# Row sums as two columns, inverted there and spread by two turns; masked scores kept in PSUM; the tail in another order

## What is computed

```
q, k, v   from projections; q and k through rms_norm, own q and k through rope
scores  = q @ [k_ctx, k_self]^T                 (causal on the 256 own keys)
weights = softmax(scores / sqrt(128))           (max over the 4352 keys subtracted)
out     = weights @ [v_ctx, v_self];   x1 = x + concat(heads) @ wo
```

## Time and profile before

| | |
|---|---|
| Median of 3 executions | 1031.19 us (1029.86 to 1032.27) |
| The profiled execution, its own time | 1030.32 us |
| Its span, first to last instruction | 1028.3 us |
| Lies around the span | 2.0 us |
| PE busy with matmuls | 986.7 us, 96% of the span |
| DVE, ACT, POOL busy | 788.0, 586.2, 517.4 us |
| Mean granted TensorE clock | 0.995 of 2.4 GHz |

### The profile page before, as it was taken

One profiled execution on the slowest core, in us unless ns is written; L12 is line 12 of the kernel. 1 busy time (PEld: TensorE's weight loads), 2 busy tenths in 40 slices (PEclk: granted clock), 3 DMA queues, 4 the chain that ended last, 5 costly groups with the idle time before them and its releaser, 6 DMA issues.

```text
span 1028.3 us, 15218 instructions
## 1 busy us (share of the span) xinstructions
PE 986.7 (96%) x5597; PEld 856.8 (83%) x5597; DVE 788.0 (77%) x1168; ACT 586.2 (57%) x962; POOL 517.4 (50%) x481
## 2 busy tenths in 40 slices
PE   8999999998899999999999999989799999999998
PEld 7888888888888888888888888877587988888887
DVE  6645666547988888888988888889479978777775
ACT  5444434345665666656666656655279576666664
POOL 4543344330777778787777787779201032222222
PEclk9999999999999999999999999989999999999999
DMA  7647564377005020221105030040540486555540
GB/s 281 195 145 224 195 205 133 114 256 239 2 8 167 22 67 1 83 92 42 47 1 171 5 89 4 2 185 1 205 164 2 155 316 216 190 192 189 194 157 20
DMA packets 52488, 127.89 MB, mean 124 GB/s; under 512 B 3872, under 2 KB 32960, under 8 KB 50880
## 3 DMA queue, kind: packets, MB, share of 16 engines
q1 hardware_dynamic: 52416, 126.94, 36.3%
HBM read 99.64 MB, written 27.30 MB: 123 GB/s over the span
## 4 chain that ended last, share of the span: by engine, by line
PE 76%; DVE 17%; issue 3%; POOL 2%; DMA 1%; ACT 0%; DVEq 0%; SPq 0%; POOLq 0%
PE bank L523 17%; PE bank L627 13%; PE bank L505 13%; PE bank L597 12%; PE bank L905 9%; DVE run_max L1065 5%; PE bank L907 5%; DVE run_max L1055 4%; DVE weights L1085 3%; POOL run_sum L1864 2%; PE bank L713 1%; PE bank L532 1%; DVE run_max L1062 1%; DMA w_xa<-in_w_in 1%; DVE weights L1052 1%
## 5 line engine op out<-in xcount | busy, mean ns | idle before, releaser
L1864 POOL TENSOR_TENSOR run_sum<-run_sum,weights 128x512 f32<-128x512 f32 x224 | 292.9, 1307 | 52.2 <-ACT weights L1581 32.7
L627 PE MATMUL bank<-weights,vN 128*128 128x256 f32 (+1 forms) x1088 | 316.2, 378 | 0.0
L597 PE MATMUL bank<-qT_hi,kT 128*128 128x256 f32 (+1 forms) x1088 | 300.9, 360 | 2.1 <-ACT weights L1577 1.2
L597 PEld LDWEIGHTS bank<-qT_hi,kT 128*128 128x128 f32 x1088 | 198.4, 189 | 25.9 <-issue 2.4
L1577 ACT COPY weights<-bank 128x512 f32<-128x512 f32 x256 | 148.8, 585 | 123.0 <-PE bank L597 114.0
L1065 DVE TENSOR_TENSOR run_max<-bank,run_max 128x512 f32<-128x512 f32 x200 | 137.2, 686 | 55.8 <-ACT weights L1577 55.4
L627 PEld LDWEIGHTS bank<-weights,vN 128*128 128x128 f32 x1088 | 173.0, 190 | 4.2
L1581 ACT ACTIVATE weights<-weights 128x1024 f32<-128x1024 f32 x144 | 144.0, 1001 | 54.8 <-DVE weights L1085 54.8
L1085 DVE TENSOR_TENSOR weights<-weights,bank 128x1024 f32<-128x1024 f32 x128 | 154.8, 1210 | 3.2 <-PE bank L655 3.2
L597 PE MATMUL bank<-qT_lo,kT 128*128 128x256 f32 (+1 forms) x544 | 153.4, 282 | 0.0
L523 PE MATMUL bank<-w_ctx_hi,ctx_hl 128*128 128x512 f32 x512 | 144.5, 393 | 1.5 <-ACT w_ctx_hi L1543 1.3
(11 more groups left out here) (236 smaller groups left out, 1514.3 us busy)
## 6 DMA issues: line engine op xcount, KB each, us to landing
e_raw<-in_experts SPq DMA_DIRECT2D x51, 768.0 KB, 4.4
k_spill<-k_stage SPq DMA_DIRECT2D x16, 1024.0 KB, 5.3
kT<-k_spill SPq DMA_DIRECT2D x15, 1024.0 KB, 5.2
v_spill<-v_stage SPq DMA_DIRECT2D x16, 512.0 KB, 6.4
vN<-v_spill SPq DMA_DIRECT2D x16, 512.0 KB, 3.6
ctx_raw<-in_ctx SPq DMA_DIRECT2D x15, 512.0 KB, 4.1
w_raw<-in_w_qkv SPq DMA_DIRECT2D x6, 1024.0 KB, 5.1
wo_sb<-in_wo SPq DMA_DIRECT2D x4, 1024.0 KB, 7.8
```

The costliest lines, as they stand in the source:

```text
L597: done = e.matmul(dst, kT[:, w, kt * P:(kt + 1) * P], qT[a][:, h, q0:L], start=m == 0, stop=m == 2)
L627: done = e.matmul(dst[:, q0:L], vN[:, kt, :].bitcast(F32), weights[:, cols], start=kt == 0, stop=kt == KTILES - 1)
L1864: e.tensor_tensor(run_sum[:, :], run_sum[:, :], here, ALU.add).then_inc(summed, 1)
```

## The change

Between the two kernels, all in the attention part and its tail:
- **Masked group**: DVE adds the mask in place in the PSUM bank, takes both maxima from there, and only then ACT copies the group to SBUF like any other (`take_scores` waits for `maxed`).
- **Order in a step on DVE**: the subtraction ahead of the running maximum; subtractions 5 and exponentials 3 steps ahead instead of 6 and 4. `fold_max` stands in the step of the head's last group instead of at k = 0 and is a reduction over the two halves instead of a `tensor_tensor`.
- **Later turns**: `turn_max`, `reduce_rows`, `spread_max` at k = 4, 5, 6 instead of 2, 3, 5 (first head: 6, 7, 8).
- **Row sums**: at k = 1 PE waits for a new ACT copy of the head's output to SBUF (`copy_out`, 128x256), then makes the sums as two columns (two fp32 products with a one-column operand); DVE inverts 128x2 at k = 2; PE spreads the two columns by two transposes at k = 3; DVE multiplies at k = 4; ACT and POOL finish at k = 5 and 6.
- **Last head's sums**: POOL adds groups 0 to 3, DVE the other 13 (`add_own_weights`), PE joins both in the sums.
- **Tail**: `w_xa`, `w_xb` and the small weights are loaded when the last head's scoring starts, `wo` in five parts while it is scored (`WO_LOADS`, `WO_ORDER`); `wo` is split from step 246 and multiplied from 249. The additions to `x` and the normalisations stand ahead of the pairs' low parts on DVE.
- Code for a split of weights that was never on (`SPLIT = {}`) is taken out.

```diff
-SUB_AHEAD, EXP_AHEAD, SPLIT_AHEAD = 6, 4, 2
+SUB_AHEAD, EXP_AHEAD, FINISH_LAG = 5, 3, 2
+TURN_AT, REDUCE_AT, SPREAD_AT = (6, 4), (7, 5), (8, 6)
-WO_STEP, WO_PRODUCTS = 250, 253
+OWN_SUMS = 4
+WO_STEP, WO_PRODUCTS = 246, 249
+WO_LOADS = (((0, 2), (9, 10)), ((2, 4), (10, 12)), ((4, 6), (12, 14)), ((6, 8), (14, 16)), ((8, 9),))
+WO_ORDER = (0, 1, 9, 2, 3, 10, 11, 4, 5, 12, 13, 6, 7, 14, 8, 15)
...
             def sum_weights(h):
-                pe.wait_ge(summed, SUMS * (h + 1))
-                e.matmul(bank[VALUE_BANKS[h % 2]][:, L:2 * L], ones[:, :], both_sum[:, :], start=True, stop=True).then_inc(sum_all, 1)
+                pe.wait_ge(out_copied, h + 1)
+                parts = [(both_sum, (summed, SUMS * (h + 1) if h < H15 else SUMS * H15 + OWN_SUMS))]
+                if h == H15:
+                    parts.append((own_both, (own_summed, SUMS - OWN_SUMS)))
...
+                for qt in range(TT):
+                    for i, (part, ready) in enumerate(parts):
+                        done = e.matmul(bank[VALUE_BANKS[h % 2]][:, L + qt:L + qt + 1], part[:, qt * P:(qt + 1) * P], ones[:, 0:1],
+                                        start=i == 0, stop=i == len(parts) - 1)
+                done.then_inc(sum_all, 1)
+            def spread_sums(h):
+                pe.wait_ge(ho, 2 * h + 1)
+                for qt in range(TT):
+                    done = e.transpose(bank[VALUE_BANKS[h % 2]][:, L + qt * P:L + (qt + 1) * P], rden[:, qt:qt + 1].to_broadcast([P, P]), ident[:, :])
+                done.then_inc(sum_all, 1)
...
                 h, k = divmod(n - NG, NG)
-                if k == 0 and h in range(H15):
+                if k == 1 and h in range(H15):
                     sum_weights(h)
+                if k == 3 and h in range(H15):
+                    spread_sums(h)
...
             sum_weights(H15)
-            for h in range(5):
+            project_out(1, 0)
+            project_out(1, 1)
+            spread_sums(H15)
+            for h in range(2, 5):
                 project_out(1, h)
             project_out(0, H15)
...
                 if g == SELF:
-                    wait_slot(dve, h, g)
-                    e.tensor_tensor(slot[:, g, 0:L + P], src[:, 0:L + P], causal[:, :], ALU.add).then_inc(maxed, 1)
+                    dve.wait_ge(scored, s + 1)
+                    e.tensor_tensor(here[:, 0:L + P], here[:, 0:L + P], causal[:, :], ALU.add).then_inc(maxed, 1)
                     for k, (to, lo, n) in enumerate(((0, 0, L), (P, L, P))):
...
-                        e.tensor_tensor(run_max[:, to:to + n], run_max[:, to:to + n], slot[:, g, lo:lo + n], ALU.max).then_inc(maxed, 1)
+                        e.tensor_tensor(run_max[:, to:to + n], here[:, lo:lo + n], run_max[:, to:to + n], ALU.max).then_inc(maxed, 1)
...
-                e.tensor_tensor(both_max[:, :], run_max[:, 0:L], run_max[:, L:2 * L], ALU.max).then_inc(maxed, 1)
+                e.tensor_reduce(out=both_max[:, :], in_=run_max[:, :].rearrange("p (t q) -> p q t", t=2), axis=AX, op=ALU.max).then_inc(maxed, 1)
...
+            def invert_sums(h):
+                dve.wait_ge(sum_all, 2 * h + 1)
...
+                e.reciprocal(rden[:, :], bank[VALUE_BANKS[h % 2]][:, L:L + 2]).then_inc(ho, 1)
             def finish_head(h):
...
-                e.tensor_tensor(head_out[z][:, :], bank[VALUE_BANKS[z]][:, 0:L], rden_all[:, :], ALU.mult).then_inc(ho, 1)
+                e.tensor_tensor(head_out[z][:, :], raw_out[:, :], bank[VALUE_BANKS[z]][:, L:2 * L], ALU.mult).then_inc(ho, 1)
...
-            for n in range(len(PAIRS)):
-                dve.wait_ge(wx_hi_done, n + 1)
-                e.tensor_tensor(pair_weights(n, 1), pair_weights(n, None), pair_weights(n, 0), ALU.subtract).then_inc(wx_lo_done, 1)
-            for tt in range(TT):
+            for tt, pairs in enumerate(((0, 1), (2, 3, 4))):
                 dve.wait_ge(wo_done, tt + 1)
                 e.tensor_tensor(x_sb[:, tt, :], x_sb[:, tt, :], bank[tt][:, :], ALU.add).then_inc(x1, 1)
                 dve.wait_ge(x1, tt + 1)
                 layernorm(2 + tt, tt, un)
+                for n in pairs:
+                    dve.wait_ge(wx_hi_done, n + 1)
+                    e.tensor_tensor(pair_weights(n, 1), pair_weights(n, None), pair_weights(n, 0), ALU.subtract).then_inc(wx_lo_done, 1)
...
+            def copy_out(h):
+                act.wait_ge(pv, NG * (h + 1))
+                if h:
+                    act.wait_ge(ho, 2 * h)
+                e.copy(raw_out[:, :], bank[VALUE_BANKS[h % 2]][:, 0:L]).then_inc(out_copied, 1)
...
                 take_scores(s)
                 for h, j in quads_at(n + EXP_AHEAD):
                     exponential(h, j)
                 h, k = divmod(n - NG, NG)
-                if k == 2 and h in range(H15):
+                if k == 1 and h in range(H15):
+                    copy_out(h)
+                if k == FINISH_LAG + 3 and h in range(H15):
                     finish_head(h)
...
             for s in range(NH * NG):
                 h, g = plan.groups[s]
+                if s == NG * H15:
+                    load_later()
+                if h == H15 and (g % 4 == 3 or g == SELF):
+                    sp.wait_ge(scored, s + 1)
+                    for lo, hi in WO_LOADS[g // 4]:
+                        e.dma_start(wo_sb[:, lo:hi, :], t["wo"][:, lo:hi]).then_inc(wo_in[g // 4] if g < SELF else w_xb_in, 16)
```

More of the change, by code:

```diff
@@ L146, in summed_at @@
     return SUMS * h + max(g, 1) + (1 if g == SELF else 0)
-def split_tiles(i):
-    return sum(1 for t in range(i) if t // BT in SPLIT)
 def quads_at(n):
@@ L242, in build_program @@
         k_stage = [back.take(f"k_stage{i}", [NKV, 2, BATCH], F32R) for i in range(2)]
-        v_stage = [back.take(f"v_stage{i}", [NKV, 2, BT, HD], F32R) for i in range(2)]
+        v_stage = [back.take(f"v_stage{i}", [NKV, BT, HD]) for i in range(2)]
         qreg = region["q"]
@@ L259, in build_program @@
         sp_ = region["spare"]
-        pT = [reg.take(f"pT{i}", [2, GW], F32R) for i, reg in enumerate([region["pt"]] * 3 + [sp_])]
         run_max = sp_.take("run_max", [GW])
+        run_sum = sp_.take("run_sum", [GW])
+        pt_ = region["pt"].again()
+        own_sum = pt_.take("own_sum", [GW])
+        own_both = pt_.take("own_both", [L])
+        rden = pt_.take("rden", [2])
         both_max = sp_.take("both_max", [L])
@@ L416, in wait_score_bank @@
             h, g = plan.groups[s]
-            if g == SELF:
-                port.wait_ge(maxed, plan.masked[h])
-            elif s % NG and s >= LEAD:
+            port.wait_ge(taken, s + 1)
+            if s % NG and s >= LEAD:
                 port.wait_ge(maxed, plan.maxed[s])
-            else:
-                port.wait_ge(taken, plan.taken[s])
         def wait_score_bank_at_end(port, b):
@@ L630, in weigh, with in_turns @@
                     yield
-            def in_turns(scores, values, n):
-                total = BT * (3 if n % NG in SPLIT else 1)
-                pulled = 0
+            def in_turns(scores, values):
                 for k, _ in enumerate(scores):
-                    while pulled < (k + 1) * total // 6:
+                    if k % 3 == 2:
                         next(values, None)
-                        pulled += 1
                 for _ in values:
@@ L1139, in dve_program @@
                 h, k = divmod(s - NG, NG)
-                if k == 3 and h in range(NH):
+                if k == REDUCE_AT[h > 0] and h in range(NH):
                     reduce_rows(h)
@@ L1507, in after @@
                     act.wait_ge(wc_lo, 2 * KD)
[L1508 to L1509 removed]
+                e.copy(v_stage[slot][:, :, s, :], bank[2 + z][:, :].rearrange("p (g d) -> p g d", g=NKV)).then_inc(v_copied, 1)
             def split_w(c):
@@ L1571, in take_scores @@
             def take_scores(s):
-                if s >= NH * NG or plan.groups[s][1] == SELF:
+                if s >= NH * NG:
                     return
                 h, g = plan.groups[s]
-                act.wait_ge(scored, s + 1)
+                if g == SELF:
+                    act.wait_ge(maxed, plan.maxed[s])
+                else:
+                    act.wait_ge(scored, s + 1)
                 wait_slot(act, h, g)
-                e.copy(s_buf[h % 2][:, g, :], bank[SCORE_BANKS[s % len(SCORE_BANKS)]][:, :]).then_inc(taken, 1)
+                e.copy(s_buf[h % 2][:, g, 0:width(g)], bank[SCORE_BANKS[s % len(SCORE_BANKS)]][:, 0:width(g)]).then_inc(taken, 1)
             def exponential(h, j):
```

286 lines of the change are left out of this document (115 added, 171 removed).

## The result

The changed kernel takes **1040.1 us** (median of 4, 1039.1 to 1044.2), the kernel before, run beside it, 1031.5 us. The ratio is 1.0093, 95% interval [1.0063, 1.0123]: slower by about 9 us, where 5.5 us faster was forecast. 1040.1 is also above the top of the range, 1035. The profiled execution took 1039.1 us.

What follows compares the result with a forecast made beforehand. PE was taken to set the pace. Heads 2.5, first head 0.2, tail -6.6 and -2.2, given back 0.6 sum to -5.5 us: profiled 1030.3 becomes 1024.8, median 1025.7 us; range 1016 to 1035.

Steps and rivals of the forecast that it cites:

- the row sums' hole: At k = 1 of every head PE waits for ACT's `copy_out`, behind a scores copy and an exponential: 1.85 us.
- the first rival: Half clock after every head's hole, losing 21 to 42 us over 14 heads: 1046 to 1067 us; chance 0.08.
- The turns: Steady heads: PE's waits at `turn_max` and `spread_max` go, gaining 0.98 + 0.9 = 1.88 us a head.
- the terms of the sum: Per steady head: loses 1.88 + 0.43, gets 1.85 + 0.44 + 0.2, so +0.18 us; times 14, +2.5 us.
- DVE still late at `spread_max`: Rival: the 0.3 us margin at `spread_max` fails, costing 0.3 to 0.7 us a head: 1030 to 1036 us; chance 0.12.
- The first head: The 1.38 us wait at `turn_max` goes, but the masked group's bank frees later and the first value step waits: net +0.2 us.
- Tail, to the last value product: From the last score to the last value product: 45.4 us becomes 38.8, gain 6.6 us, bounds 4 and 8.
- 15 steps of a value step and a head's products: Tail after `spread_max`: steps of 1.55 us, held up a little by DVE from head 8 on, ending at 31.9 us.
- Tail, to the pairs: From the last value product to the pairs' products: 30.4 us becomes 28.2, gain 2.2 us, bounds 0 and 5.
- forecast new hole of 3.4 us: Ahead of the last sums PE waits for DVE's share, ready about 42.2 us behind the last score; half clock adds 2.2 us.
- The tokens' hole: The 5.71 us hole before the pairs, ended by the normalised tokens, was to go: no wait for the tokens.
- Given back: DVE reaches the state-space block's first steps 1.7 us later relative to PE: +0.6 us, range 0 to 1.7.

Runs made afterwards that it cites:

- Experiment 3: Changed kernel with four unused fp32 products of 256 columns on PE ahead of the row sums, filling the hole; 1020.0 us.
- experiment 1: Changed kernel with ACT's copy of a head's output one step earlier, at k = 0 instead of k = 1; 996.7 us.
- experiment 10: Experiment 1 with, in the first head alone, ACT copying the masked group right behind the mask and DVE taking both maxima from SBUF; 996.6 us.
- Experiments 11 and 12: Experiment 1 with head 14's row sums and all that follows them later: by three steps 1000.1 us, by one step 998.3 us.
- experiment 9: Experiment 1 with the pairs' large weights again loaded only behind the last sums and DVE making the pairs' low parts before `x`; 1006.8 us.
- experiment 2: Changed kernel with ACT's copy of the head's output ahead of the exponential in the same step k = 1; 1008.5 us.
- experiment 5: Changed kernel with two unused fp32 products of 256 columns on PE ahead of the row sums; 1021.0 us.
- experiment 4: Changed kernel with one unused fp32 product of 256 columns on PE ahead of the row sums; 1021.5 us.
- experiment 8: Changed kernel with one more ACT copy ahead of the awaited copy and one more PE product ahead of the row sums, heads 0 to 13; 1038.5 us.
- experiment 6: Changed kernel with one more unused ACT copy of 128x256 ahead of the copy PE waits for; 1043.3 us.
- experiment 7: Changed kernel with three more ACT copies of 128x256 ahead of the copy PE waits for, heads 0 to 13; 1058.0 us.

## Why the prediction was wrong

**The step that failed** is the pricing of the row sums' hole: "PE stands 1.85 us at every head", entered into the sum as +1.85 and nothing behind it, with the reason, under the first rival, that "two holes a head left it at 1.00". The hole was right in place, cause and size. That it would leave the clock at 1.00 was taken from heads whose holes showed 0.74 and 0.71, half as long. Behind the new hole, 1.46 by the same measure, half clock came in 11 of 14 heads at 1.6 us each. Experiment 3 shows the clock alone to be worth 20 us, head 14's fall included, experiment 1 hole and clock 43.4. (The terms listed for the hole add up to 1.77 and 0.06, so 1.83 and not 1.85; experiment 1 measures 1.82.) The rival was named, with 0.08, and with the right price for one head (1.5 to 3 us). Two things were wrong in it: the chance, and that it knew only "in none" or "in every head", 1046 to 1067 us. The measured 1040 lies between its cases because 3 heads were spared. The nearest evidence had been a hole of 1.38 without half clock and one of 2.84 with it; a hole of 1.46 is close above the first, but it is one observation, and there were to be fourteen trials. The price of being wrong, 20 us, was more than the whole forecast gain.

The Trainium skill, "TensorE: Matmul & The Clock Gate", section "A second HAM failure mode: psum-queue depth-cycling", was cited for a kernel whose short idles between groups of matmuls send the clock to and fro. In kind this trace agrees: the clock goes to 1.2 GHz and back once a head, 11 times. The prediction set it aside on the strength of the earlier trace rows, and was wrong to.

**The turns** gained what was forecast. No wait stands before `turn_max` or `spread_max` in a steady head, and the head without the new hole takes 27.5 to 27.7 us (experiment 1), against 29.3 + 0.18 - 1.85 = 27.6 by the terms of the sum. DVE's new operations are as estimated, in the groups by line (busy us, mean ns, idle before):

```profile
L1026 DVE TENSOR_REDUCE both_max<-run_max 128x256 f32<-128x512 f32 x16 | 11.2, 700 | 0.5
L1008 DVE TENSOR_TENSOR bank<-bank,causal 128x384 f32<-128x384 f32 x16 | 9.0, 566 | 5.7 <-PE bank L553 5.7
L1011 DVE TENSOR_TENSOR run_max<-bank,run_max 128x256 f32<-128x256 f32 x16 | 6.8, 424 | 0.5
...
L1011 DVE TENSOR_TENSOR run_max<-bank,run_max 128x128 f32<-128x128 f32 x16 | 4.7, 291 | 0.6
L1068 DVE RECIPROCAL rden<-bank 128x2 f32<-128x2 f32 x16 | 2.6, 161 | 1.4 <-PE bank L608 1.2
```

The fold takes 0.70 us where 0.7 was taken and 0.42 to 1.3 allowed. The note on cachelines of the Trainium skill, "SBUF — State Buffer", has a penalty for each access that crosses to a new 16-byte line. The prediction put the fold by that rule near its own upper bound of 1.3; the measurement decides, and it shows no such penalty for this read, as another reduction of 512 elements in this kernel (L940) takes 676 ns. The rival "DVE still late at `spread_max`" did not happen in a steady head.

**The first head** was forecast at +0.2. The longer hold on the masked group's bank was seen, "0.42 + 0.28 + 0.5 = 1.2 us later", and 2.06 - 0.87 = 1.19 is what it measures, against this row of the kernel before, TensorE at the same place:

```profile
249.33 0.48 PE L597 MATMUL bank<-qT_hi,kT 128*128 128x256 f32 x2 [0.87 <-DVE weights L1052]
```

Half clock behind it was not foreseen, 3 us of it; it cost only 0.2, by experiment 10.

**Tail, to the last value product**: gain 3.0 for 6.6. The step that failed is the term "15 steps of a value step and a head's products", which follows DVE and leaves out POOL. POOL still adds head 14 when PE runs value products alone, at 11.82 / 7 = 1.69 us a group against PE's 0.86, so its fold for head 14 is late:

```profile
705.13 11.82 POOL L1849 TENSOR_TENSOR run_sum<-run_sum,weights 128x512 f32<-128x512 f32 x7
717.10 1.89 POOL L1853 TENSOR_TENSOR run_sum<-run_sum,weights 128x256 f32<-128x256 f32 x2
719.07 0.73 POOL L1834 TENSOR_TENSOR both_sum<-run_sum 128x256 f32<-128x256 f32 x1
```

2.20 us of hole and about 1.6 of half clock are 3.8, against 3.6 missing. Experiments 11 and 12 put a limit on that reading: removing this hole alone gains nothing, since DVE then makes PE wait at the end. (The sum was also slightly off by itself: 8.8 and 15 steps of 1.55 are 32.05 before any hold-up by DVE, not 31.9.)

**Tail, to the pairs**: gain 7.3 for 2.2. The forecast new hole of 3.4 us is 0.60, because PE came 3.6 us later to it, and so the 2.2 of half clock behind it fell away: 28.2 - 2.8 - 2.2 = 23.2, measured 23.1. DVE itself was ready 43.0 us behind the last score, close to the 42.2 put down; luck has a part in that, as the terms listed for it add up to 10.9 + 20.2 + 9.1 = 40.2 only, and the low parts of `wo` took 1.01 us each for 1.26. The tokens' hole is gone for the reason given; experiment 9 brings it back. The two tail errors are one: the sum to the pairs, 67.0 forecast, is 65.5.

**Given back**: 0.2 for 0.6.

**The sum, mended.** To the last scores: the forecast 2.7, 17.6 for the heads' half clock, 0.2 for the first head's, less 14 x (29.48 - 29.40) = 1.1 for the steady head. Another 1.1 go ahead of all that was priced: the first score starts at 235.07 us before and at 233.97 after, and in the runs of the experiments anywhere from 233.46 to 234.71. That makes 18.3 us, for 19.1 measured; the 0.8 us between them are not placed. Behind the last scores: -8.8 forecast, -10.3 measured, and 0.4 less given back.

## What to carry to other kernels

Where one engine is the bound, price a new hole on TensorE twice, for its length and for the clock behind it, and treat holes longer than any that the trace shows as harmless as a case of their own with a real chance. When an engine waits for a copy, look in the copying engine's list for what stands ahead of it in the same step: one step earlier was worth 43 us here. Ask of each fall of the clock whether another engine would have made TensorE wait anyway: in the first head it cost 0.2 us, in a steady head 1.6. If a wait can't be removed, shorten it or fill it; useless work in the hole made this kernel 20 us faster. And follow every engine through the stretch where the loop's rhythm changes, the ones that were never the bound above all.

## What the runs showed of the hardware

Half clock behind a head's hole, by its bracket and by the period of a head without half clock, 14 heads each, each row from one profiled execution:

| bracket, us | period, us | heads at half clock | from |
|---|---|---|---|
| 0.52 | 28.5 | 0 | experiment 2 |
| 0.60 | 29.4 | 0 | experiment 5 |
| 1.03 | 29.4 | 0 | experiment 4 |
| 1.46 | 29.4 | 11 | the changed kernel |
| 1.46 | 29.85 | 7 | experiment 8 |
| 1.90 | 29.85 | 9 | experiment 6 |
| 2.77 | 30.7 | 3 (more in the other three) | experiment 7 |

Unexpected were four things. The step between 1.03 and 1.46 us is sharp, 0 of 14 to 11 of 14. Beyond it the share does not rise with the length. Holes beyond it can leave the clock at 1.00: eleven of 2.77 us in experiment 7, one of 2.17 in the first head of experiment 10. And the same hole in the same program can go either way. In the first head the hole of 2.04 to 2.06 us, with all work before it alike, was followed by a clock of 0.50 to 0.57 from 250 to 253 us in eight kernels (the changed one and experiments 1, 2, 3, 7, 8, 11 and 12) and of 1.00 in four (4, 5, 6 and 9). At the sums of head 14 a hole of 1.80 us left the clock at 1.00 in experiment 4, and one of 1.76 was followed by 0.66 in experiment 8.

One fall shows as about 3.1 us at half speed and costs about 1.6 us; in experiment 7 it was up to 3.2 us (a period of 33.93 for 30.7). That something beyond the length decides is shown by these cases. That it is the time at which the hole comes is the reading that fits them all; what would set that time was not measured.
